# Causal attention on row tiles of 32 rows in plain fp32, with both passes interleaved at a distance of 20 items

## The reference

```python
q = (x @ Wq.T).reshape(B, S, 16, 8).transpose(0, 2, 1, 3)   # x: layer-normed, B = 2, S = 2048
k = (x @ Wk.T).reshape(B, S, 16, 8).transpose(0, 2, 1, 3)
v = (x @ Wv.T).reshape(B, S, 16, 8).transpose(0, 2, 1, 3)
scores = q @ k.T / sqrt(8), masked where key > query
out = softmax(scores) @ v
x = x + out.reshape(B, S, 128) @ Wo.T
```

## Time and profile before

| | us |
|---|---|
| three runs, median | 5902.98 |
| profiled execution, its own time | 5908.11 |
| span of the profiled execution | 5906.1 |
| in the span: from the first projection of the causal attention (3911.48) to its last values (5265.3) | 1353.8 |
| of it: projections, splits and first stacks | 76.0 |
| first step, first pass only | 115.9 |
| seven steps with both passes | 1078.8 |
| last step, second pass only | 83.1 |

### The profile page before, as it was taken

How to read it: one execution, slowest core, us unless ns; L and a number is a source line. 1 busy time by engine, 2 the same in 40 slices (tenths; PEclk the granted TensorE clock), 3 DMA queues, 4 the chain that set the end, 5 groups by cost and what they waited for, 6 DMA issues and landing times.

```text
span 5906.1 us, 163733 instructions
## 1 busy us (share of the span) xinstructions
PE 5179.1 (88%) x71504; PEld 3133.2 (53%) x71696; DVE 3948.9 (67%) x5079; ACT 2684.4 (45%) x3457; POOL 2643.7 (45%) x947
## 2 busy tenths in 40 slices
PE   8899889988998899989998899867777887798999
PEld 5566556664666466646665566532222222246776
DVE  5988488956986588748983889437566666623333
ACT  1565445644665365535653556421444444451111
POOL 2888378845885488628881788310000000000000
PEclk7999899989999899989998999875888888888999
DMA  1111101110111011101111111020111000100000
GB/s 51 31 37 37 46 27 37 39 53 19 39 37 60 12 38 37 39 34 35 37 39 40 31 37 39 20 62 14 17 18 17 12 12 12 17 33 2 4 4 5
DMA packets 94224, 173.85 MB, mean 29 GB/s; under 512 B 23641, under 2 KB 35554, under 8 KB 91874
## 3 DMA queue, kind: packets, MB, share of 16 engines
q1 hardware_dynamic: 93538, 163.67, 10.6%
HBM read 55.71 MB, written 8.39 MB: 11 GB/s over the span
## 4 chain that ended last, share of the span: by engine, by line
PE 76%; DVE 8%; issue 5%; ACT 4%; DMA 3%; POOL 2%; SPq 1%; DVEq 0%; ACTq 0%; POOLq 0%
PE D L1127 7%; PE D L1046 6%; PE D L1061 5%; PE D L1068 5%; PE D L1191 4%; PE D L978 4%; PE D L1219 4%; PE D L1310 4%; PE D L1085 4%; PE D L1026 3%; PE D L1206 3%; PE D L1094 3%; PE D L1096 3%; PE D L1034 3%; DVE mxp L818 3%
## 5 line engine op out<-in xcount | busy, mean ns | idle before, releaser
L423 POOL TENSOR_TENSOR rn<-ss,mhalf 128x32 f32<-128x32 f32 x192 | 1212.2, 6313 | 314.3 <-DVE ss L711 312.2
L818 DVE TENSOR_REDUCE mxp<-D 128x1 f32<-128x512 f32 (+3 forms) x1280 | 722.2, 606 | 417.6 <-PE D L1194 268.9
L612 ACT ACTIVATE hh<-D 128x1024 f32<-128x1024 f32 (+1 forms) x320 | 283.8, 936 | 605.5 <-PE D L1209 477.0
L1127 PE MATMUL D<-PTb,V 64*64 64x32 f32 x24576 | 415.7, 222 | 60.2 <-issue 42.8
L769 DVE TENSOR_TENSOR TOK<-D,RA 128x1024 f32<-128x1024 f32 x384 | 466.4, 1215 | 0.0
L428 POOL TENSOR_TENSOR hh<-hh,rr 128x1024 f32<-128x1024 f32 x192 | 364.6, 1899 | 219.8 <-DVE rr L739 219.5
L432 POOL TENSOR_TENSOR XC<-XC,TOK 128x1024 f32<-128x1024 f32 x132 | 311.5, 2360 | 335.2 <-DVE TOK L769 335.0
L1127 PEld LDWEIGHTS D<-PTb,V 64*64 64x64 f32 x24576 | 396.7, 138 | 102.5 <-issue 102.1
L709 DVE TENSOR_REDUCE ss<-TOK 128x32 f32<-128x2048 f32 x192 | 436.9, 2276 | 1.1 <-POOL rn L423 1.1
L558 ACT ACTIVATE V<-D 128x512 f32<-128x512 f32 x384 | 229.3, 597 | 451.5 <-PE D L1094 384.7
L263 POOL TENSOR_TENSOR rstd<-var_s,mhalf 128x4 f32<-128x4 f32 x96 | 96.3, 1007 | 717.2 <-DVE var_s L238 717.2
(11 more groups left out here) (219 smaller groups left out, 10307.2 us busy)
## 6 DMA issues: line engine op xcount, KB each, us to landing
V<-V SPq DMA_DIRECT2D x936, 64.0 KB, 2.0
V<-V SPq DMA_DIRECT2D x192, 192.0 KB, 2.4
RA<-tabs_dram SPq DMA_DIRECT2D x6, 2048.0 KB, 7.8
RB<-watt_dram SPq DMA_DIRECT2D x6, 2048.0 KB, 12.2
parts_dram<-hh SPq DMA_DIRECT2D x48, 128.0 KB, 2.3
RA<-parts_dram SPq DMA_DIRECT2D x12, 384.0 KB
TOK<-parts_dram SPq DMA_DIRECT2D x36, 128.0 KB
RB<-parts_dram SPq DMA_DIRECT2D x12, 384.0 KB
```

The costliest lines, as they stand in the source:

```text
L423: pool.tensor_tensor(rn[:, st % 2, :], ss[:, :], mhalf[:, :], ALU.pow).then_inc(s["powed"], 1)
L612: act.activation(PTE[n % 2][:, 2 * half:2 * half + 2, 0:CH - r * P], ST2[half][:, :, 0:CH - r * P], ACT.Exp, scale=float(HD) ** -0.5)\
L818: dve.tensor_reduce(mxp[:, h, qt, kc:kc + 1], PB[2 + n % 2][:, 0:first_pass_keys(qt, kc)], AX.X, ALU.max).then_inc(s["max1"], 1)
L1127: m = pe.matmul(D01[64 * h:64 * h + 64, at:at + WIN], VW[n % 2][ks, (0 if r % 2 else 2) + h, p * DH:(p + 1) * DH], PTb[ks, p * P + 32 * r: ...
```

## The change

**Row tiles in fp32.** The splits, the scratch tensor, the stacks and their loads are gone. `project_group` projects queries and keys of one group (4 heads) with weights that are padded with zeros to 32 columns a head, so that head h of the group lands in rows 32h to 32h + 7 of `QK[g % 3]`. ScalarE copies the projection out (`copy_qk`); for keys it adds a vector that puts a one into row 32h + 8. For queries, row 32h + 8 gets minus the maximum by a DMA (`max_rows`), now in fp32 and once for each chunk of 512 queries. Scores are fp32 matmuls with 8 rows (first pass) or 9 rows (second pass), each head on its own strip of 32 rows of the array.

**Units.** Two heads make a unit: F is a unit of the first pass, S of the second; the number behind is the pair of heads (0: heads 0 and 1, 1: heads 2 and 3). All units go through three pairs of banks in turn (`PAIR`: D01, D23, D67), and a unit waits until the third unit before it has been read, by VectorE (`max1`) or by ScalarE (`exp2`). One iteration of TensorE's list is S0, F1, S1, F0, then the values of the item before. The second pass is 20 items (`LAG`) behind the first, across the borders of groups, so that there are 20 iterations with F alone, 300 with both, 20 with S alone.

**Other moves.** The mask of the second pass is cut on GpSimd after the exponential (`cut_diagonal`, 128 times on 128 x 4 x 128). The projections of groups 1 to 7 stand within the loop, eight a group, one in four iterations; each goes through PB[5]. Maxima are turned and negated once a chunk (32 times) instead of once a group in three parts. The copy of the output moves from VectorE to ScalarE (`copy_o`), and one division writes four blocks. The loops are written out in full, so every wait is against a constant.

```diff
-        QST = [r[:, :].bitcast(bf16) for r in (RA, RB)]
-        KST = [TOK[:, :, :].rearrange("p a b -> p (a b)").bitcast(bf16), XC[:, :].bitcast(bf16)]
+        WQK = OTb[:, 0, :].rearrange("p (a g n) -> p a g n", a=2, g=4)
+        QK = [[r[:, 0:SEQ], r[:, SEQ:2 * SEQ]] for r in (RA[:, :], RB[:, :], XS)]
-        PTE = [hh[:, 0:4, :], V2[:, :, :]]
+        PTE = [hh[:, 0:4, :], V2[:, :, :], V3[:, :, :]]
+        PAIR = [D01, D23, D67]
+        LAG = 20
...
+        def released_by(unit):
+            m = UNIT_NO[unit] - 3
+            if m < 0:
+                return None, 0
+            kind, at, hp = UNITS[m]
+            return ("exp2", 2 * (at - LAG) + hp + 1) if kind == "S" else ("max1", 2 * at + 2 - hp)
...
 (pool)
+            def cut_diagonal(i):
+                pool.wait_ge(s["exp2"], 2 * i + 2)
+                pool.affine_select(out=PTE[i % 3][:, :, 0:P], in_=PTE[i % 3][:, :, 0:P], compare_op=ALU.is_ge, fill=0.0, base=0,
+                                   pattern=[[0, GH], [1, P]], channel_multiplier=-1).then_inc(s["diag_cut"], 1)
...
 (act)
+            def copy_qk(g, c, qk):
+                act.wait_ge(s["qk_proj"], g * 8 + 2 * c + qk + 1)
+                dst = QK[g % 3][qk][:, c * CH:(c + 1) * CH]
+                if qk == 0:
+                    act.activation(dst, PB[5], ACT.Copy).then_inc(s["qk_copied"], 1)
+                else:
+                    act.activation(dst, PB[5], ACT.Identity, bias=ones_row).then_inc(s["qk_copied"], 1)
...
 (dve)
-                dve.tensor_reduce(mxp[:, h, qt, kc:kc + 1], PB[2 + n % 2][:, 0:first_pass_keys(qt, kc)],
-                                  AX.X, ALU.max).then_inc(s["max1"], 1)
+                dve.tensor_reduce(mxp[:, 2 * hp:2 * hp + 2, qt, kc],
+                                  pair_of(("F", at, hp))[:, :].rearrange("p (h n) -> p h n", h=2)[:, :, 0:keys], AX.X, ALU.max)\
+                   .then_inc(s["max1"], 1)
...
 (pe)
+            def project_group(g, c, qk):
+                hg, b = divmod(g, 2)
+                if misc["qk_copied"]:
+                    misc_free()
+                pe.matmul(PB[5], WQK[:, qk, hg, :], chunk(XC, b * CB + c), start=True, stop=True).then_inc(s["qk_proj"], 1)
+                misc["qk_copied"] += 1
...
-                m = pe.matmul(bank[:, 0:keys], QST[p][0:KR, h * SEQ + qt * P:h * SEQ + (qt + 1) * P],
-                              KST[p][0:KR, h * SEQ + kc * CH:h * SEQ + kc * CH + keys], start=True, stop=not diag)
+                for x in range(2):
+                    rows = slice(32 * (2 * hp + x), 32 * (2 * hp + x) + HD)
+                    m = pe.matmul(banks[:, x * CH:x * CH + keys], QK[g % 3][0][rows, qt * P:(qt + 1) * P],
+                                  QK[g % 3][1][rows, kc * CH:kc * CH + keys], start=True, stop=not diag)
...
+                for x in range(2):
+                    rows = slice(32 * (2 * hp + x), 32 * (2 * hp + x) + HD + 1)
+                    m = pe.matmul(banks[:, x * CH:x * CH + CH - r * P], QK[g % 3][1][rows, kt * P:(kt + 1) * P],
+                                  QK[g % 3][0][rows, c * CH + r * P:(c + 1) * CH], start=True, stop=True)
...
+            for at in range(TOTAL + LAG + 4):
+                i = at - LAG
+                if 0 <= i < TOTAL:
+                    second_scores(i, 0)
+                if at < TOTAL:
+                    first_pass(at, 1)
+                if 0 <= i < TOTAL:
+                    second_scores(i, 1)
+                if at < TOTAL:
+                    first_pass(at, 0)
+                if 1 <= i <= TOTAL:
+                    second_values(i - 1)
+                if chunk_end(at - 2) is not None:
+                    turn_max(chunk_end(at - 2))
+                if chunk_end(i - 3) is not None:
+                    turn_o(chunk_end(i - 3))
+                if proj_at(at) is not None:
+                    project_group(*proj_at(at))
```

More of the change, by code:

```diff
@@ L339, in _ @@
                     straddling_windows(l, n)
+            sp.wait_ge(s["y_added"], DEPTH * NB)
             sp.dma_start(wC[:, :, :], t["wC"]).then_inc(s["w1att_in"], 16)
[L342 to L375, removed]
-                load_stacks(0, i)
-                max_rows(0, 2 * i)
-                sp.wait_ge(s["pv2"], (2 * i) * ITEMS + 2)
-                load_stacks(1, i)
@@ L380, in _, with max_rows @@
-            max_rows(1, NG - 1)
-            sp.wait_ge(s["pv2"], NG * ITEMS + 2)
+            sp.dma_start(WQK, t["wqk"]).then_inc(s["w1att_in"], 16)
+            def max_rows(cg):
+                g, c = divmod(cg, CB)
+                sp.wait_ge(s["neg_copied"], cg + 1)
+                for h in range(GH):
+                    sp.dma_start(QK[g % 3][0][32 * h + HD:32 * h + HD + 1, c * CH:(c + 1) * CH].rearrange("r (x n) -> r x n", n=P),
+                                 nT[4 * h:4 * h + 4, cg % 2, :]).then_inc(s[f"neg_rows{cg % 2}"], 16)
@@ L382, in _ @@
+            for cg in range(CHUNKS):
+                max_rows(cg)
+            sp.wait_ge(s["pv2"], TOTAL)
             sp.dma_start(EW1, t["ew1"].rearrange("e p n -> p e n")).then_inc(s["moew_in"], 16)
@@ L897, in _ @@
+            for at in range(TOTAL + LAG + 4):
+                if at < TOTAL:
+                    first_max(at, 1)
+                    first_max(at, 0)
+                if chunk_end(at) is not None:
+                    chunk_max(chunk_end(at))
+                if chunk_end(at - 2) is not None:
+                    negate_max(chunk_end(at - 2))
+                if chunk_end(at - LAG - 3) is not None:
+                    store_o(chunk_end(at - LAG - 3))
             for c in range(NC):
@@ L1262, in _ @@
-            pe.sem_inc(s["pv2"], 2)
-            att_step(0, 0, 1, None, True, False)
-            with pe.Fori(1, NG // 2) as i:
-                att_step(2 * i - 1, 1, i, i)
-                att_step(2 * i, 0, i + 1, i)
-            att_step(NG - 1, 1, NG // 2, NG // 2)
-            att_step(NG, 0, None, NG // 2, False, True)
-            pe.wait_ge(s["o_stored"], NG * CB + 1)
+                misc["o_stored"] += 1
+            for c in range(CB):
+                for qk in range(2):
+                    project_group(0, c, qk)
@@ new lines, in _ @@
+            for c in range(NC):
+                if c >= 2:
+                    pe.wait_ge(s["c_vcopy"], c - 1)
+                for b in range(NBLK):
+                    m = pe.matmul(PB[6 + c % 2][:, b * P:(b + 1) * P], XC[:, c * CH + b * P:c * CH + (b + 1) * P], wC[:, 0, :],
+                                  start=True, stop=True)
+                m.then_inc(s["c_proj"], 1)
+            pe.wait_ge(s["tri_ready"], 2)
+            pe.wait_ge(s["o_zero"], 1)
+            pe.wait_ge(s["c_vcopy"], NC)
```

388 lines of the change are left out of this document (161 added, 227 removed).

## The result

| | us |
|---|---|
| kernel before, median of 4 runs | 5899.38 (5891.22 to 5903.97) |
| kernel after, median of 4 runs | 6729.84 (6727.78 to 6737.27) |
| ratio | 1.1412, 95% interval 1.1392 to 1.1431 |
| predicted | 5921, range 5800 to 6080 |

A forecast was written before the change was run, and what follows sets the result against it. It took the chain of waits S0, exponential, F0, values to bound the stage: 25 + 44 + 1250 + 40 = 1359 against 1353.8 us, plus about 8 for the clock, +13 on 5908.1: 5921 us, range 5800 to 6080.

The forecast's parts named there:

- about 8 us: Causal attention stage: the clock is at half only once, for the first 10 us, costing about 8 us.
- rival C: Stretch with both passes: clock stays at 1.2 GHz, S0, F0 and values take twice as long, 660 us, 6580; chance 13%.
- the first pass alone: 20 items with F only, before the second pass joins: VectorE bounds, 44 us with 4 projections.
- the chain: One full-width iteration with both passes: S0, exponential, F0, values in turn, 4.28 us with weights, switches and wake-ups.
- side by side: Scores: matmuls on different strips run together, a unit of two heads takes 0.86 us, and F1 runs beside S0.
- B: Scores: F1 doesn't run beside S0; if units don't overlap at all, 90 us more, 6011; chance 12%.
- D: Scores: strips of 32 rows run one after another, an iteration takes 7.1 us, 975 us more, 6896; chance 3%.
- case A: Before S0, before F0, between F0 and values: weights and switches are hidden, 93 us in 300 iterations, 5828; chance 22%.
- preparation: Before the loop: eight projections of group 0, values of eight chunks, last copy and slow clock at first, 25 us.
- both: 300 iterations with both passes: 1155 us, plus projections 56, output transpositions 30 and turned maxima 9, about 1250.
- the end: Second pass alone, 17 units: TensorE 36 us, ScalarE 36, with the turns 40.
- the covers: GpSimd's cut, gather, reductions, copies and `max_rows` stay hidden; one failing would cost 100 us at most.

The follow-up runs named there:

- single heads: Changed kernel with scores on all 32 rows, taken one head and one bank at a time over six banks instead of pairs: 5989.53 us, ratio 1.0147.
- the six kernels of the table above: Changed kernel by score rows, first/second pass: 8/9 6729.84 us; 8/9 with added full matmuls 6856.92; 16/16 6672.51; 8/32 6337.46; 32/9 6267.86; 32/32 5943.26.

## Why the prediction was wrong, point by point

- **The step that failed is the clock.** The sum prices every link at 2.4 GHz and sets "about 8 us" aside for a slow clock, and the prediction held against rival C that "TensorE streams in 3.4 of 4.28 us, 4.0 with the ends, which is nearer to the 96% busy of the step that held the full clock". That argument took busy time for what the clock follows. The matmuls of the step in the earlier trace rows took 72 to 75 rows or all 128, as the earlier trace rows show, and the new ones take 8 and 9 on each strip, as the diff shows. The runs put 787 us in the place of 8. The prediction had named the half-used array as a reason for C, and then gave the other argument more weight. It also counted strips and not the rows used within them: with the same strips and 32 rows in each the clock is 1.00.
- **C's own price was too low.** 660 us came from three streams in an item. Weights, projections, masks, turns and the first pass alone slow down too: a full item costs 2.75 us more and not 2.6 (7.10 - 4.35), and the four parts of the stage 784 us more (2176 - 1392) and not 660.
- **Right: the chain.** S0, exponential, F0, values, 4.28 worked out, 4.35 at full clock. The 0.07 are one term: ScalarE starts 0.11 us after S0's last record ends (4060.86 + 0.59 to 4061.56), where I took 0.04 from VectorE's row.
- **Right: side by side.** F1 with S0; neither B nor D. With single heads four strips start within 0.02 us (from 4039.06 on), their second records 0.54 later and the next round's 0.97 later, which is 0.86 of streaming and 0.10 of weights: four streams in the time of one. The Trainium skill (TensorE: Matmul & The Clock Gate, Measured speedup vs the span model) has 3.07 times for four, the reason for 66 us in rival B; nothing of that loss is seen here.
- **Right: no case A in this order.** At full clock weights and switches cost what the rows said (links of 1.08, 1.06 and 0.98 us against 1.07, 1.07 and 0.98).
- **Off by a little, in the same direction:** with 32 rows preparation 31 (25), the first pass alone 55 (44), both 1260 (1250), the end 46 (40). Together 33 us over, less the 8 us set aside for a slow clock, and the rest of the span was 4 us shorter (5940.4 - 1392 = 4548): 21 of the 22 us from 5921 to 5943. The first pass alone was priced as VectorE's work at full clock; TensorE was busy for 53.76 of its 55 us, at a mean clock of 0.65.
- **Right: the covers.** GpSimd's cut takes 0.64 us (128 x 512 elements; bounds were 0.29 and 2.36), 128 times, and nothing waits for it in the full item; two groups of values in the last step do, 1.0 us together. No DMA stands in the chain (0%).
- **The range.** Most of C was left outside on purpose, at 13%. The chance was too low for what the trace had: what spoke for it (a first pass alone at half clock while 75% busy, rows half used) was evidence from this trace, and what spoke against it was a likeness of busy shares.

The Trainium skill (TensorE: Matmul & The Clock Gate, What's actually happening) says that the gate is set by how busy TensorE has been, the array being throttled by default. By that rule a stretch at 100% busy runs at the full clock. The trace of after doesn't agree: 2035.5 of 2036 us busy, clock 0.52. The measurement decides: the trace's busy time alone does not tell the clock, and of the six kernels of the table above the ones with more rows in their scores ran at the higher clock.

What stays open: whether it is rows, cells of the array (the scores take 128 columns each, the values 9 on four strips) or something that goes with them. No run varied the columns of the weights, and none gave more rows to the weights alone or to the streamed operand alone.

## What to carry to other kernels

A matmul on few rows of a strip costs as much time as one on 32 rows at the same clock, and can cost twice as much by what it does to the clock; where short contractions fill a long stretch, pad the rows with zeros. Read PEclk together with the rows in the PE lines, not with the busy share: a TensorE at 100% and 0.5 is slow, not full. When a new order is priced, price the items on the diagonal and those with extra work too: the full item fell by 9% and the kernel got slower.

## What the runs showed of the hardware that was not expected

- Zeros count for the clock. The added rows held zeros (the first pass's one row of ones met zeros too), every product in them was zero, and the clock went from 0.52 to 1.00.
- With one pass on 32 rows the clock goes back and forth: the same full item takes anything from 4.34 to 7.1 us in one run, at a mean clock of 0.70 to 0.75.
- The tail of the changed kernel recovered by itself at 9 rows: with the second pass alone the clock over 6040 to 6087 is 0.80, half level at first and full behind it, where beside the first pass it was 0.52. S0 and S1 run on all four strips together there, but that can't be the reason alone: with single heads on 8 and 9 rows four strips ran together too, at 0.52. What differs as well is the share of the values, which take all 128 rows. In the tail they have 1.83 of the 3.85 us of an item (they start at 6051.77, the next scores at 6053.60, the next values at 6055.62), in the full item of the stretch 1.83 of 7.10. No run tests that by itself.
